# Spreading a scale's chain over the rounds of a linear-attention stage

## What is computed

```python
# linear attention (8 heads of 64)
qkv = einsum('bnd,ed->bne', x, w_qkv)
k, v = instance_norm(k), instance_norm(v)      # over the 64 of a head
dots = einsum('bhnd,bhne->bhde', k, v)
out = einsum('bhnd,bhde->bhne', q, dots) / N
out = einsum('bne,de->bnd', out, w_out) + b_out
# graph convolution
h = relu(layer_norm(x) * gamma + beta)
return (segment_sum(h[src], dst) / degree) @ W_l.T + b_l + h @ W_r.T
```

## Time and profile before

| what | value |
|---|---|
| median of 3 runs | 1848.53 us (1844.95 to 1850.83) |
| the profiled execution's own time | 1841.18 us |
| its span, first to last instruction | 1839.4 us |
| busy, share of the span: PE, DVE, ACT, POOL | 91%, 52%, 36%, 13% |
| mean granted clock of TensorE | 0.962 |

### The profile page before, as it was taken

How to read it: one execution, slowest core, us unless ns; L and a number is a source line. 1 busy time by engine, 2 the same in 40 slices (tenths; PEclk the granted TensorE clock), 3 DMA queues, 4 the chain that set the end, 5 groups by cost and what they waited for, 6 DMA issues and landing times. The chain is left out here.

```text
span 1839.4 us, 31351 instructions
## 1 busy us (share of the span) xinstructions
PE 1673.8 (91%) x9423; PEld 1104.2 (60%) x9424; DVE 959.2 (52%) x2786; ACT 668.2 (36%) x1347; POOL 235.4 (13%) x290
## 2 busy tenths in 40 slices
PE   6888998888989899998898999999996989996998
PEld 5344555666757323333665899999763558544667
DVE  8988888887468663344502000000156863235862
ACT  4023445673124575664212334343312423001220
POOL 2000000001010005700052000000163001300102
PEclk9999999999999999999699999999997989997989
DMA  2001112226550000000525113113130001341001
GB/s 84 0 15 58 59 58 87 116 116 220 179 161 1 1 1 1 1 1 1 190 72 180 55 63 111 63 66 106 32 93 9 1 1 58 101 129 38 1 0 59
DMA packets 86408, 118.86 MB, mean 65 GB/s; under 512 B 6788, under 2 KB 72510, under 8 KB 86176
## 3 DMA queue, kind: packets, MB, share of 16 engines
q1 hardware_dynamic: 80992, 106.53, 17.2%
q0 software_dynamic: 3936, 10.37, 1.8%
q10 hardware_dynamic: 1376, 0.66, 0.1%
HBM read 70.66 MB, written 46.87 MB: 64 GB/s over the span
## 5 line engine op out<-in xcount | busy, mean ns | idle before, releaser
L786 PE MATMUL bank<-onehot_key,onehot_low 128*128 128x320 bf16 x1304 | 222.0, 302 | 38.5 <-DVE onehot_low L585 23.9
L581 DVE TENSOR_SCALAR onehot_key<-iota_keys,edge_keys 128x640 bf16<-128x640 f16 x652 | 231.6, 382 | 25.4 <-PE bank L786 20.8
L786 PEld LDWEIGHTS bank<-onehot_key,onehot_low 128*128 128x128 bf16 x1304 | 103.6, 98 | 147.2 <-DVE onehot_key L581 54.6
L1880 ACT ACTIVATE hidden<-bank,b_cols 128x128 f32<-128x128 f32 x344 | 126.3, 367 | 178.5 <-PE bank L1807 155.0
L1961 DVE TENSOR_TENSOR slot_columns<-bank,b_rows 128x256 f32 x43 | 18.3, 425 | 290.5 <-PE bank L1813 290.5
L1807 PEld LDWEIGHTS bank<-slot_columns,w 128*128 128x128 f32 x1376 | 163.1, 195 | 5.6 <-issue 3.4
L1807 PE MATMUL bank<-slot_columns,w 128*128 x1376 | 163.4, 278 | 3.2 <-issue 3.2
L1813 PE MATMUL bank<-w,hidden 128*128 128x256 f32 x688 | 155.6, 379 | 0.0
L1813 PEld LDWEIGHTS bank<-w,hidden 128*128 128x128 f32 x688 | 127.4, 190 | 15.5
L653 ACT ACTIVATE edge_low_shifted<-edge_low,window_offset 128x631 f32 x81 | 66.7, 823 | 191.1 <-DVE onehot_low L585 190.3
L1597 ACT ACTIVATE XT<-bank 128x512 f32<-128x512 f32 x160 | 84.3, 603 | 57.8 <-PE bank L1525 57.8
(11 more groups left out here) (498 smaller groups left out, 2735.2 us busy)
## 6 DMA issues: line engine op xcount, KB each, us to landing
AT_dram<-at_strip SPq DMA_DIRECT2D x20, 640.0 KB, 4.1
A_dram<-a_strips SPq DMA_DIRECT2D x20, 640.0 KB, 2.9
sg_strip<-AT_dram SPq DMA_DIRECT2D x20, 640.0 KB, 4.0
back_strip<-A_dram SPq DMA_DIRECT2D x24, 480.0 KB, 5.0
w<-in_L_ffn_W1p SPq DMA_DIRECT2D x8, 1024.0 KB, 5.4
w<-in_L_ffn_W2p SPq DMA_DIRECT2D x8, 1024.0 KB, 7.8
slot_rows<-ty_zero SPq DMA_DIRECT2D x1, 6144.0 KB, 24.5
slot_columns<-slot_rows SPq DMA_DIRECT2D x12, 512.0 KB, 8.7
```

Of the source, the lines that this page charges most:

```text
L581: dve.tensor_scalar(ohk[:, q, :], ioh[:, :], key[:, ds(chunk(n, offset, q), 1)], None, ALU.is_equal).then_inc(s_key[q], 1)
L786: last = pe.matmul(bank[2 * (x % 2) + h][:, 0:HB], ohl[q // 2][:, :, q % 2], ohk[:, q, h * HB:(h + 1) * HB], start=False, stop=q == Q - 1, ...
L1880: act.activation(hid[:, f, 0:P], bank[f % 4][:, 0:P], ACT.Gelu, bias=b1[:, ds((e + 1) * FB + f, 1)]).then_inc(s_rg, 1)
```

## The change

The chain's instructions are the same, in the same order among themselves. Each piece moves behind the work of one of the tiles on its engine: PE's product behind dots(3); ACT's two squares behind tile 2 and its roots behind tile 7; DVE's maximum and sum behind tile 4, the maximum of the product and the bound behind tile 5, the rest behind tile 8. No DMA is issued by any of them, and no buffer is added.

```diff
 # PE
                         for t in range(DEEP - 1):
                             kv(t)
-                        pe.wait_ge(s_wq, 1)
-                        for c in range(CB):
-                            last = pe.matmul(bank[7][:, 0:C], onesf[:, :], wsq[:, c, :], start=c == 0, stop=c == CB - 1)
-                        last.then_inc(s_wn, 1)
                         for t in range(T):
                             if t + DEEP - 1 < T:
                                 kv(t + DEEP - 1)
                             dots(t)
+                            if t == 3:
+                                pe.wait_ge(s_wq, 1)
+                                for c in range(CB):
+                                    last = pe.matmul(bank[7][:, 0:C], onesf[:, :], wsq[:, c, :], start=c == 0, stop=c == CB - 1)
+                                last.then_inc(s_wn, 1)
 # ACT
-                        act.wait_ge(s_sw, 16 * 8)
-                        act.activation(wsq[:, :, :], sg_w[:, :, 0:C], ACT.Square).then_inc(s_wq, 1)
-                        act.activation(gq[:, :, :], sg_gb[:, 0:2, :], ACT.Square).then_inc(s_wq, 1)
-                        act.wait_ge(s_gm, 1)
-                        act.activation(gz[:, 3:6], gz[:, 0:3], ACT.Sqrt).then_inc(s_gr, 1)
                         for t in range(T):
...
                             act.activation(ss[k][:, 0, :], ss[k][:, 1, :], ACT.Sqrt).then_inc(s_rt, 1)
+                            if t == 2:
+                                act.wait_ge(s_sw, 16 * 8)
+                                act.activation(wsq[:, :, :], sg_w[:, :, 0:C], ACT.Square).then_inc(s_wq, 1)
+                                act.activation(gq[:, :, :], sg_gb[:, 0:2, :], ACT.Square).then_inc(s_wq, 1)
+                            if t == 7:
+                                act.wait_ge(s_gm, 1)
+                                act.activation(gz[:, 3:6], gz[:, 0:3], ACT.Sqrt).then_inc(s_gr, 1)
 # DVE (the twelve lines removed in front of the loop are those added here)
                             dve.tensor_tensor(by_head(K[k][:, :]), ...).then_inc(s_k, 1)
+                            if t == 4:
+                                dve.wait_ge(s_wq, 2)
+                                dve.tensor_reduce(gz[:, 1:2], gq[:, 0, :], AX.X, ALU.max)
+                                dve.tensor_reduce(gz[:, 2:3], gq[:, 1, :], AX.X, ALU.add)
+                            if t == 5:
+                                dve.wait_ge(s_wn, 1)
+                                st.then(dve.tensor_reduce(gz[:, 0:1], bank[7][:, 0:C], AX.X, ALU.max))
+                                dve.tensor_scalar(gz[:, 0:3], gz[:, 0:3], 1e-20, None, ALU.max).then_inc(s_gm, 1)
+                            if t == 8:
+                                dve.wait_ge(s_gr, 1)
+                                ...
+                                dve.tensor_scalar(sg_sf[:, :], indeg[:, :], gz[:, 6:7], None, ALU.mult)
+                                dve.tensor_scalar(sg_w[:, :, 0:C], sg_w[:, :, 0:C], gz[:, 7:8], None, ALU.mult)
```

More of the change, by code:

```diff
@@ L2196, in _ @@
                         st = Steps(dve, s_ch)
[L2197 to L2208, removed]
                         for t in range(T):
@@ L2221, in _ @@
                             dve.tensor_tensor(by_head(K[k][:, :]), by_head(bank[KV[t % DEEP][0]][:, :]), spread(ss[k][:, 2, 0:Hh], 2, Dh), ALU.mult).then_inc(s_k, 1)
+                            if t == 4:
[8 more added lines that the diff above has]
+                                dve.wait_ge(s_gr, 1)
+                                st.then(dve.scalar_tensor_tensor(out=gz[:, 6:7], in0=gz[:, 4:5], scalar=float(C) ** 0.5, in1=gz[:, 5:6], op0=ALU.mult, op1=ALU.add))
+                                st.then(dve.scalar_tensor_tensor(out=gz[:, 6:7], in0=gz[:, 6:7], scalar=1.0 / (HALF_SCALE * C ** 0.5), in1=gz[:, 3:4], op0=ALU.mult, op1=ALU.mult))
+                                st.then(dve.reciprocal(gz[:, 7:8], gz[:, 6:7]))
+                                dve.tensor_scalar(sg_sf[:, :], indeg[:, :], gz[:, 6:7], None, ALU.mult)
+                                dve.tensor_scalar(sg_w[:, :, 0:C], sg_w[:, :, 0:C], gz[:, 7:8], None, ALU.mult)
                         dve.wait_ge(s_use, T)
```

## The result

The median of 11 runs is 1836.87 us (1834.33 to 1845.01), against 1848.28 us of 11 runs of before: a ratio of 0.9949, interval 0.9933 to 0.9965, so 6.5 to 12.4 us faster. The profiled execution took 1835.62 us, its span is 1833.9.

The account below looks back on a forecast made before the run. DVE and ACT in the chain delay tile 0, and from dots(1) PE bounds the stage. Hold 2.82 plus clock 0.93 less product 0.86 gives 2.9 us; 1848.53 - 2.9 = 1845.6 us, range 1840.5 to 1849.5.

Parts of the forecast that it names:

- The view of what bounds the stage: DVE and ACT in the chain delay tile 0; from dots(1) the stage is PE's, at 4.33 us a round.
- The hold on L2213: DVE's small instruction of tile 0 waits to the end of POOL's stream, ending at 1410.87, not 1413.69: 2.82 us won.
- rows 7 and 8: Profile rows: beside POOL's L902, of 7 additions, two instructions took 0.96 and 0.60 us, each waiting at most one addition.
- The turns: Rival at tile 0: DVE's small instructions each wait for one POOL addition at most; 6.4 us won, 1842.1 us, chance 0.30.
- PE's idle time and the clock: In front of dots(0): 2.8 us idle, not 4.75; then 3.4 us at half clock cost 1.7, so 0.93 won.
- the forecast's own case: Full hold at tile 0 and low clock behind PE's idle time: 2.9 us won, 1845.6 us, chance 0.40.
- the hold is full and the clock stays: Rival at tile 0 and dots(0): full hold, full clock afterwards; 4.6 us won, 1843.9 us, chance 0.12.
- rows 10: Profile rows a stage later: after 3.0 us of PE idle time the clock stood at 0.50 for 3.4 us.
- PE's product: Behind dots(3), where PE never waits, the moved product loses 0.86 us.
- The covers: Behind tile 2, K of tile 3 comes 1.8 us before dots(3); from tile 4 DVE leads by at least 2 us.
- DVE's and ACT's pieces: Moved work behind tiles 2 to 8, covered, costs nothing; uncovered, DVE's would be 2.8 us; ACT's squares are 1.24 us.
- The last term: For the whole kernel, 2.9 us are taken from the median, 1848.53, not the profiled execution, 7.4 us under it.

Follow-up runs that it names:

- e_early: The kernel after, but ACT's two squares and PE's product stay in front as in before, only the waiting steps moved; ratio 0.9949 (0.9933 to 0.9965).
- e_tail: The kernel after, with PE's product in front of the last dots and the rest of the chain behind the loop, POOL's stream unchanged; ratio 0.9957 (0.9941 to 0.9973).
- e_port_size: No computation: a small tensor_scalar beside streams of 40 additions (128 or 256 columns) or 12 (512); held up to 18.5 us in a stream of 40.
- e_pool_before: The kernel before, with each of POOL's 20 additions to X held back until K of its tile is written; ratio 0.9986 (0.9972 to 1.0000).
- e_warm: The kernel before, with nine matmuls of zeros added in PE's idle time in front of dots(0); ratio 0.9994 (0.9977 to 1.0010).

## Why the prediction was wrong

- **The view of what bounds the stage held.** DVE and ACT in front of tile 0, a PE-bound loop behind it, the rounds of 4.33 us: all of it is in the profile after.
- **"The hold on L2213": this is the step that failed.** I bounded it by nothing and by 4.7 us, and took the high end, "since L2202 is the nearest row in place". It measured 0.20 us over its free duration (0.37 in all), and 0.39 in the second execution, against 4.7. The rows 7 and 8 were the better guide, because what they share with tile 0 is not the stream but the place: few additions had been made. Those of rows 7 stood beside a stream of seven, L2202 beside the 17th of twenty. I had both cases in the trace and read the difference as one of streams. Yet the hold was no fiction: in e_early and e_tail the same instruction was held to the stream's end, and dots(0) came 14.06 and 14.05 us behind the first matmul, just where the forecast had it (1413.24 less 1399.18). Tile 0 comes to the place at which either happens. Nothing in the rows of before could tell which, and that both profiles of after drew the short wait is partly luck.
- **The turns came as the rival had them**: 0.64 to 0.80 us on five instructions, K of tile 0 at 1412.98 less 1401.21, so 11.8 us behind the first matmul; the rival's 1411.4 less 1399.2 is 12.2. Its 6.4 us lack the 0.9 of the loop's tail, where I had named no effect of the clock. By the Trainium skill ("SBUF — State Buffer", Who interferes with whom) whoever issues first has the shared pair for its whole instruction and the other blocks. Read as a wait for that one instruction, the trace of after agrees, at 0.65 us. L2202, e_early and e_port_size, at 2.5, 4.6 and 18.5 us, differ from it, and there the measurement decides.
- **PE's idle time and the clock**: 0.78 us in place of 2.8, the clock stayed, and 2.53 us came back in place of 0.93. This term was not safe in the forecast's own case either. The price, 1.7 us for a short idle time, was 1.8 us in e_pool_before, but e_tail had the full hold and 2.45 us of idle time and paid nothing. That is the rival "the hold is full and the clock stays". I had one row, rows 10, and took it as the rule.
- **PE's product**: 0.86 us, as forecast.
- **The covers held.** No wait for la_k from dots(1) to the last kv; DVE's and ACT's pieces cost nothing.
- **The size of the miss in the stage.** 2.9 us were forecast and 7.7 came: 2.2 more from the hold (5.06 for 2.82), 1.6 from the clock behind dots(0), 0.9 from the tail.
- **The last term was the scatter.** I set the forecast against the median of three runs and left the scatter out of the range. A stage that is 7.7 and 7.1 us shorter gave medians 11.4 and 7.0 us lower in two sets. The range's low end, 1840.5, was made for a gain of 7.4 and no scatter.

## What to carry to other kernels

A chain of tiny steps with three hand-overs between engines costs its waiting, not its work: put each piece behind work that its engine has anyway, and where PE has to wait in any case, put PE's piece there. When DVE works beside a row of back-to-back instructions on GpSimd, do not take one contested duration as the price: find out how many instructions of the row had been issued by then, and break a long row with a wait per tile. In the traces DVE's small instructions of tile 0 then take 0.17 us again; in before this was worth 2.6 us by the ratio (with an interval that reaches zero), in after the ratio did not change. A gap on PE that closes can give back the clock behind it too, here 2.5 us beside the 5.1 by which dots(0) moved; a gap of 2.4 us cost 1.8 us in one kernel and nothing in another, so price it as a range.

## What the runs showed of the hardware that I had not expected

- The first small VectorE instruction (tensor_scalar in SBUF) to come beside back-to-back GpSimd additions of 256 columns waits for one of them up to the 11th in a row, and from the 15th on for all that are left; between them it goes either way, and the longest hold seen, 18.5 us, was one of these. For 128 columns the change is between the 12th and the 14th, for 512 at the 10th.
- Behind an instruction that has just had its turn, others got theirs up to the 19th addition (0.64 to 0.65 us each in after, 0.65 at the 17th in e_warm).
- PE's idle time of 2.41 us was followed by a clock of 0.50 in e_pool_before, and one of 2.45 us by 1.00 in e_tail.
- The scatter of the whole kernel, 1841 to 1852 us for before, lies for the most part outside this stage: of 10.1 us between two profiled executions 6.8 lie ahead of it and 3.1 behind the loop. It goes with the mean granted clock (0.962 and 0.956).
